# Two batches sorted ahead of the expert tiles, a first table of seven batches, and a reordered warm-up

## The reference

```python
h = _layernorm(x, gamma, beta);  x1 = conv(h) + x          # conv: complex decaying scan over the tokens
h = jax.nn.silu(_layernorm(x1, gamma, beta) @ w1 + b1) @ w2 + b2
x2 = x + h + x1                                             # 128 -> 512 -> 128
t = _layernorm(x2)
topk_logits, topk_idx = jax.lax.top_k(t @ router.T, 2);  probs = softmax(topk_logits)
out = x2 + sum over the two experts e of probs[e] * (gelu(t @ w1[e].T + b1[e]) @ w2[e].T + b2[e])   # 128 -> 256 -> 128
```

## Time and profile before

| | us |
|---|---|
| median of 3 runs | 493.84 (491.52 to 494.1) |
| the profiled execution | 490.28 |
| its span, first to last instruction | 488.5 |
| busy in it: PE, DVE, ACT, POOL | 392.7, 357.6, 320.1, 268.5 |
| granted TensorE clock, mean | 0.933 |

### The profile page before, as it was taken

The page is one execution under the profiler, slowest core; times in us unless marked ns, Lnnn a source line. Parts: engine busy times, 40 slices in busy tenths (PEclk is TensorE's granted clock), DMA queues, the critical chain, the costliest instruction groups (busy, mean ns, idle before and its releaser), DMA issues.

```text
span 488.5 us, 11387 instructions
## 1 busy us (share of the span) xinstructions
PE 392.7 (80%) x2812; PEld 346.4 (71%) x2812; DVE 357.6 (73%) x1329; ACT 320.1 (66%) x773; POOL 268.5 (55%) x331
## 2 busy tenths in 40 slices
PE   1354199799798899888977778499999999999990
PEld 1221168597777687868766667499999999999990
DVE  7999999969999999981625545456767666666770
ACT  5781479878878788865545533267776777777750
POOL 6960844726787886666252155645545454545451
PEclk9986589989999999999988887979999999999996
DMA  7658000000111111112023123324333333333200
GB/s 258 175 169 292 0 2 0 1 1 2 47 46 36 58 47 46 47 48 91 2 91 98 42 92 97 113 78 122 96 86 100 95 103 99 98 94 107 73 11 0
DMA packets 33284, 37.42 MB, mean 77 GB/s; under 512 B 5255, under 2 KB 29332, under 8 KB 33093
## 3 DMA queue, kind: packets, MB, share of 16 engines
q1 hardware_dynamic: 27236, 23.56, 16.6%
q0 software_dynamic: 5984, 13.13, 7.8%
HBM read 19.52 MB, written 18.92 MB: 79 GB/s over the span
## 4 chain that ended last, share of the span: by engine, by line
PE 49%; DVE 21%; issue 7%; ACT 7%; POOL 4%; another core or an unknown queue 2%; ACTq 0%; POOLq 0%; DVEq 0%
PE up_p L985 16%; PE up_p L1002 8%; PE down_p L1002 8%; PE down_p L829 5%; DVE stats L1088 4%; PE turn_p L801 3%; ACT rows L658 3%; ACT work L631 2%; PE down_p L994 2%; DVE work L1152 2%; POOL sorted_rows L560 2%; DVE work L1150 2%; PE route_p L867 2%; DVE mom L1094 2%
## 5 line engine op out<-in xcount | busy, mean ns | idle before, releaser
L588 POOL DMA_INDIRECT out<-result,out_id x91 | 89.3, 981 | 100.6 <-DVE result L1466 56.7
L760 ACT ACTIVATE hid_t<-up_p 128x512 f32<-128x512 f32 x91 | 54.3, 597 | 75.7 <-PE up_p L985 55.1
L985 PE MATMUL up_p<-xt,work 128*128 128x128 f32 x728 | 101.9, 285 | 1.3 <-ACT work L775 0.8
L560 POOL DMA_INDIRECT sorted_rows<-rows,pos x64 | 76.9, 1202 | 39.9 <-DVE pos L1207 22.6
L985 PEld LDWEIGHTS up_p<-xt,work 128*128 128x128 f32 x728 | 92.8, 199 | 3.1 <-ACT xt L755 1.7
L775 ACT ACTIVATE work<-mw_c 128x256 f32 x182 | 65.9, 417 | 0.9 <-issue 0.9
L829 PEld LDWEIGHTS down_p<-w_sb,work 128*128 128x128 f32 x512 | 60.5, 192 | 5.0 <-issue 4.8
L829 PE MATMUL down_p<-w_sb,work 128*128 128x128 f32 x512 | 63.5, 277 | 0.0
L618 ACT ACTIVATE work<-up_p,b_all 128x512 f32<-128x512 f32 x64 | 41.3, 681 | 17.3 <-PE up_p L815 14.1
L801 PE MATMUL turn_p<-ident,work 128*128 128x128 f32 x192 | 28.0, 294 | 30.5 <-ACT work L644 12.3
L1002 PE MATMUL down_p<-mw_sb,hid_t 128*128 x368 | 51.8, 286 | 0.9 <-issue 0.9
(11 more groups left out here) (237 smaller groups left out, 784.3 us busy)
## 6 DMA issues: line engine op xcount, KB each, us to landing
tin<-sorted_rows SPq DMA_DIRECT2D x91, 136.0 KB
resid<-in_x SPq DMA_DIRECT2D x8, 512.0 KB, 3.8
sorted_rows<-zeros SPq DMA_DIRECT2D x29, 136.0 KB, 2.2
out<-result,out_id POOLq DMA_INDIRECT x91
work<-in_mw SPq DMA_DIRECT2D x1, 1024.0 KB, 6.1
sorted_rows<-rows,pos POOLq DMA_INDIRECT x64
work<-in_w SPq DMA_DIRECT2D x1, 256.0 KB
w_sb<-in_w SPq DMA_DIRECT2D x1, 256.0 KB
```

The costliest lines, as they stand in the source:

```text
L560: g.indirect_dma_start(sorted_dram, bass.IndirectOffsetOnAxis(pos[b % 2][:, j:j + 1], 0), rows[b % ROWBUFS][:, j, :], None).then_inc(s_sor ...
L588: g.indirect_dma_start(out_rows, bass.IndirectOffsetOnAxis(out_id[k][:, :], 0), result[k][:, :], None, bounds_check=TOKENS - 1, oob_is_err ...
L760: s_.activation(hid_t[s % 2][:, :], mid_p[s % 2][:, :], ACT.Gelu).then_inc(s_gelu, 1)
L985: last = t.matmul(mid_p[s % 2][:, c * TILE:(c + 1) * TILE], ring[s % RING][:, c * 128:(c + 1) * 128], xt[s % 2][:, :], start=True, stop=True)
```

## The change

`EARLY_BATCHES` is 7, so that `EARLY` is (7 x 1024 - 28 x 127) // 128 = 28. Each engine's loop ends with iteration 6. What iteration 7 held is written out, together with the choice of batch 6 and the turn, routing and choice of batch 7, before the tiles. The first table is made from seven batches, and SP waits before tile 0 for the rows of seven. Only `place(7)`, `positions(7)`, the probabilities of 7, its sort and the second table stay between the tiles. In the warm-up `convolution(0)` goes ahead of `weights()`, `x1_sum(0)` and the moments of batch 2 ahead of both rotations of batch 1, and `low(0)` between the scans and the products of batch 1. `pair_facts()` goes from behind iteration 0 into the written-out part.

```diff
-EARLY_BATCHES = 6
+EARLY_BATCHES = 7
 class Tail:
-            norm = 0
-            choose_sixth = 0
 ...
+            tanh = 0
+            place = -1
+            positions = 0
+            counts = 2
+            sums = 3
+            facts = 4
+            sort = 2
+            apart = 2
 # GpSimd
-            for i in range(LAST + 1):
+            for i in range(LAST):
                 iteration(i)
+            x2_scales(LAST - 1)
+            sort_rows(LAST - 2, range(TPB))
+            sort_rows(LAST - 1, range(0, 3))
+            x2_scales(LAST)
+            sort_rows(LAST - 1, range(3, TPB))
 ...
+            for s in range(TILES):
+                store(s)
+                k, rest = divmod(s - Tail.sort, Tail.apart)
+                if 0 <= k < TPB and rest == 0:
                     sort_rows(LAST, range(k, k + 1))
 # ScalarE, after iteration 6
+            silu_act(LAST, 0)
+            silu_act(LAST, 1)
+            x2_norm(LAST - 1)
+            probabilities(LAST - 2)
+            silu_act(LAST, 2)
+            xm_copy(LAST - 1)
+            silu_act(LAST, 3)
+            probabilities(LAST - 1)
             load_table(ACT.Gelu, 1)
 ...
+            x2_norm(LAST)
+            for s in range(2):
+                weights(s)
+            xm_copy(LAST)
+            weights(2)
 # VectorE, warm-up
+            convolution(0)
             weights()
-            convolution(0)
-            rotated = rotate_re(1)
             x1_sum(0)
+            x_moments(2, x_statistics(2))
+            rotated = rotate_re(1)
             rotate_im(1)
-            x_moments(2, x_statistics(2))
-            scans(1, rotated)
-            low(0)
+            scans(1, rotated, lambda: low(0))
 ...
 # VectorE, after iteration 6
+            x2_sum(LAST - 1)
+            x2_stats(LAST - 1)
+            choose(LAST - 2)
+            positions(LAST - 2)
             pair_facts()
+            choose(LAST - 1)
+            x2_sum(LAST)
+            positions(LAST - 1)
+            tile_numbers(0)
+            x2_stats(LAST)
+            tile_windows(0)
+            tile_table(0)
+            choose(LAST)
```

More of the change, by code:

```diff
@@ L747, in _ @@
             a.wait_ge(s_b1, 1)
-            for i in range(0, LAST + 1):
+            for i in range(0, LAST):
                 iteration(i)
+            silu_act(LAST, 0)
[6 more added lines that the diff above has]
+            probabilities(LAST - 1)
             load_table(ACT.Gelu, 1)
@@ L783, in _ @@
                     x_copy(s + 3)
[L784 to L790, removed]
+                    if s >= 0:
+                        weights(s + 3)
                 if s == Tail.tanh:
@@ L973, in _ @@
             pe.wait_ge(s_folded, 6)
-            for i in range(0, LAST + 1):
+            for i in range(0, LAST):
                 iteration(i)
+            mlp_up(LAST, 0)
+            mlp_up(LAST, 1)
+            mlp_down(LAST, 0)
+            mlp_up(LAST, 2)
+            place(LAST - 2)
+            xm_turn(LAST - 1)
+            mlp_down(LAST, 1)
+            mlp_up(LAST, 3)
+            route(LAST - 1)
+            mlp_down(LAST, 2)
+            mlp_down(LAST, 3)
+            place(LAST - 1)
+            tile_counts(0)
+            tile_sums(0)
+            tile_facts(0)
+            xm_turn(LAST)
+            route(LAST)
             def tile_up(s):
@@ L1028, in _ @@
                     at[s + 1] = experts_of(s + 1)
[L1029 to L1034, removed]
                 if s == Tail.place:
@@ L1144, in rotate_im, with scans @@
                 d.tensor_tensor(vi, u, in_im, ALU.mult).then_inc(s_ui, 1)
-            def scans(b, rotated):
+            def scans(b, rotated, between=None):
                 decay = decay_factor.to_broadcast([128, LENGTH])
@@ L1152, in scans @@
                 d.tensor_tensor_scan(vi, decay, vi, start_v[:, 1:2], ALU.mult, ALU.add).then_inc(s_vi, 1)
+                if between:
+                    between()
                 then(d.tensor_tensor(vr, vr, out_re, ALU.mult))
@@ L1410, in _ @@
             scans(0, rotated)
+            convolution(0)
             weights()
-            convolution(0)
+            x1_sum(0)
+            x_moments(2, x_statistics(2))
             rotated = rotate_re(1)
-            x1_sum(0)
             rotate_im(1)
-            x_moments(2, x_statistics(2))
-            scans(1, rotated)
-            low(0)
+            scans(1, rotated, lambda: low(0))
             convolution(1)
@@ L1421, in _ @@
             iteration(0)
-            pair_facts()
-            for i in range(1, LAST + 1):
-                iteration(i)
+            for i in range(1, LAST):
+                iteration(i)
+            x2_sum(LAST - 1)
+            x2_stats(LAST - 1)
+            choose(LAST - 2)
+            positions(LAST - 2)
+            pair_facts()
+            choose(LAST - 1)
[6 more added lines that the diff above has]
+            choose(LAST)
             def experts_of(s):
@@ L1482, in _ @@
                     second_bias(s + 1)
[L1483 to L1488, removed]
                 if s == Tail.positions:
```

20 lines of the change are left out of this document (1 added, 19 removed).

## The result

The changed kernel takes **488.0 us** (median of 14 runs, 485.84 to 492.05), the kernel before 491.26 (14 runs beside them, 488.09 to 494.1): ratio 0.994, 95% interval 0.9911 to 0.9969. The profiled execution took 488.62 us (before: 490.28), its span is 486.8, the mean granted clock 0.923.

A forecast was written before the change was run, and what follows sets the result against it. DVE was taken to bound the batch loop and PE the tile loop, with 32.0 us excess between them. Tail -15.3 and warm-up -1.7 make -17.0, from 493.84 to 476.8 us; range 470 to 488.

The forecast's parts named there:

- Some of the late signals ... I take 3 us: Between tiles, PE's late signals were to cost 3 us, within bounds of 0 and 20, with eight sorts left of sixteen.
- the first rival: Late signals between tiles follow the sorts: half the sorts leave 10 us instead of 3, so 483.8; chance 0.24.
- Only where POOL issues sorts and stores in turn: From 280 to 320 us, PE's signals were said to come late only under this mixed issue; no separate size.
- the slower rival: Late signals fall in the serial stretch before tile 0: four on the path cost 20 us, so 497; chance 0.05.
- Tile 0's result at 276.9: Start of the tiles at DVE: 278.6 by the tail's steps, set by POOL's sorts ending at 267.1, less 1.7 of warm-up.
- The routing of batch 7: Before tile 0, beside the sorts' path: routing to end at 269.0 and `choose(7)` at 273.2, hidden since `place(7)` is wanted about 274.5.
- Settled loop and second table: From tile 0 to 90: 90 periods, 178.5 us, plus 0.8 for the second table and 0.5 for low clock.
- The warm-up: Before iteration 0, the new order was to gain 1.7 us (bounds 0.5 and 2.5), PE's first dense matmul near 59.
- The starved start: Rival for the serial stretch: POOL's sorts run at their mean pace, 3.8 us later, so 480.6; chance 0.08.
- All comes back: Rival: 17 us more than taken, 493.8, no change, needing eight sorts to do what sixteen did; chance 0.07.
- The 9 us of low clock: In the stretch between batch and tile loops, PE's clock losses were to shrink from about 9 us to 2.
- The base: The runs' median, 493.84 us, 3.6 above the profiled execution, from which the 17.0 us were subtracted.

The follow-up runs named there:

- burst, no stores: Changed kernel with batch 7's eight sorts in a row ahead of tile 0's result and stores of tiles 0 to 27 left out: 487.33 us, 0.987 of before.
- Kept busy, 11: Changed kernel with 11 extra 128x512 matmuls that nobody reads, in PE's gaps ahead of tile 0: 486.88 us, 0.9929 of the kernel before.
- the warm-up alone: Kernel before with only the warm-up's new order: 494.95 us, 1.0006 of the kernel before.
- the tail alone: Changed kernel with the old warm-up order: 494.72 us, 1.0042 of the kernel before.
- sorts first: Changed kernel with all eight sorts of batch 7 ahead of the first store: 485.75 us, 0.9875 of the kernel before.

## Why the prediction was wrong

- **"Some of the late signals ... I take 3 us"**: this is the step that failed. The eight sorts cost 10.8 us (up to 14.4 in other executions). The mechanism was named (PE's signals come late where POOL mixes sorts and stores), its size was taken from the wrong row: the settled loop has no sorts in it. Eight scatters did more than half of what sixteen did, the first rival's rule (10 us). That rival with the start as late as it was gives 483.8 + 5.2 = 489.0, against 488.0 measured.
- **Its description was wrong in part.** "Only where POOL issues sorts and stores in turn": a burst alone does it too ("burst, no stores"). The argument against the slower rival, that sorts alone delay nothing in iteration 7, failed with it. In the changed kernel PE's last dense matmuls end at 249.75 + 0.94 = 250.69, behind sorts of batch 5, and DVE gets their signal for `x2_sum(7)` at 253.99 [2.68 <-remote]. The trace of the kernel before had such a case: beside the sorts of batch 4 (221.1 to 231.0) the signals of PE's matmuls that end at 228.27 and 229.96 come at 231.08 and 232.61, 2.8 and 2.7 us late, with no store in sight.
- **Tile 0's result at 276.9** (278.6 less 1.7): it came at 282.11. The last sort ends at about 268.5, 3.1 late: 0.7 stood there when batch 5's sorts began (242.42, where the forecast had 243.42 less 1.7), some 2.4 are the held signal. The other 2.0 lie between tile 0's up (274.12) and its result, 8.0 us where I had 6.0. "Kept busy, 11" has 4.55 there, so it is the low clock; but the other two executions of the changed kernel, whose clock rose earlier, have 6.3 and 6.4, so these 2.0 belong to this execution more than to the kernel.
- **The routing of batch 7**, forecast from 267.1 to 269.0, took 3.58 us. It stayed hidden: `choose(7)` ends at 276.22 and PE waits 0.19 for it.
- **Settled loop and second table**: without the sorts the first 28 tiles took 58.0, where I had 55.5 + 0.8 + 0.5 = 56.8; the last 62 took 124.1 instead of 122.9. Together 2.3. With 7.8 of the sorts (10.8 - 3.0) that is the 10.1.
- **The warm-up**: x1_sum(0) at 44.52 (forecast 44.4), the first dense matmul at 59.20 (59), but nothing in the time of the warm-up alone. At batch 5's sorts the changed kernel is 1.0 us ahead of the kernel before, and so is the tail alone with the old warm-up (242.31), so not even that 1.0 can be put down to the warm-up.
- **The starved start** didn't occur: sorts before tile 0 come every 1.26 to 1.36 us. "All comes back" is nearly what happened, by 10.1 and 5.2 us, not by one cause.
- **The 9 us of low clock** were taken as lost before and saved after. The clock stood at 0.50 from 260 to 280 instead: the idle time only moved. The Trainium skill (TensorE: Matmul & The Clock Gate, What's actually happening) puts the ramp below 1% of a typical span, which would be 4.9 us here. "Kept busy, 11" takes 3.7 us less from tile 0's turn to its result than the changed kernel (2.0 and 2.1 less than its other executions), so for this stretch the trace agrees; what the low clock costs over the whole span no run here measures.
- **The base**: the three runs' median, 493.84, lay 2.6 us above that of all 14 (491.26), of which they are three.

## What to carry to other kernels

When a wait's releaser is an unknown one, first remove the suspected traffic altogether and read the whole stretch; a share guessed from a quiet row isn't a size. Count GpSimd's indirect scatters beside short TensorE steps, and look whether they come to stand back to back: one a tile went nearly free here (58.0 us for 28 tiles that settled take 55.5), the ones above that cost 1.3 us each or more, and neither fewer bytes nor one sort in three tiles helped. Moving work into a serial stretch moves the cold clock with it.

## What the runs showed of the hardware

TensorE's signals are held for 2 to 10 us while GpSimd issues indirect scatters beside the tile loop, and then come several at once (five within 0.3 us at 292). It takes neither the data of the scatters nor their bytes; plain writes from the same engine didn't do it. The Trainium skill (TensorE: Matmul & The Clock Gate, The cost: per-tile semaphore tail) has a tail of some 26 ns for each increment of a semaphore; the held signals are beyond that by two orders, with some 6 us for tile 1 in "sorts first". Not explained: why a signal is held at all; why, in the kernel before and in the changed one, the first four bursts of eight in the batch loop (13.6 us each) hold no signal over 0.6 us, while the fifth (9.9 us) holds two by some 2.7; why the sixth, as long as the fifth, holds 3.1 in the changed kernel and 0.6 in the kernel before; and single holds of 1.7 to 2.7 us at later tiles in most of the kernels, sorts or none.
